# A fused attention and expert kernel: some key blocks' softmax sums by adding transfers, and an addition moved to GpSimd

## The chip, the cores and the metric

The kernel runs on one core of a Trainium2 chip. A time is the device time of one launch in microseconds (us); lower is better. The core has five engines that run their own instruction streams and meet at semaphores: TensorE (PE; its weight loads are shown apart as PEld), VectorE (DVE), ScalarE (ACT), GpSimd (POOL) and SyncE (SP, which only issues transfers). Sixteen DMA engines move the data. A transfer issued by SP or ScalarE is of the kind "hardware_dynamic" in the profile (queue q1 for SP), one issued by GpSimd is "software_dynamic" (queue q0).

## The reference

The kernel computes one block of a network in four parts. Only the third is touched by the change; the others matter as its neighbours.

```python
x = x + tanh(g_xattn[0]) * L0_xattn(layernorm(x), ctx, ...)      # projection and depooling
x = x + tanh(g_ffn[0])   * L0_ffn(layernorm(x), ...)             # 8 experts, top 1
# the third part: 2048 queries of 8 heads of 32 against 1601 keys
Q = split_heads(layernorm(x)) * 32 ** -0.5
K, V = split_heads(ctx[:, :256]), split_heads(ctx[:, 256:])
logits = einsum('bhqd,bhkd->bhqk', Q, K) + b + mask
x = x + tanh(g_xattn[1]) * softmax(logits) @ V
x = x + tanh(g_ffn[1])   * L1_ffn(layernorm(x), ...)             # 8 experts, top 2
```

## The kernel before

The attention is done in eight passes n = 0 to 7. A pass takes 512 queries (a group of four 128-row pieces) and four of the eight heads (hf = n % 2). The 1601 keys are 13 blocks kc of 128. In the function `interleaved`, which every engine walks through in its own way, a step is one key block of one pass, 8 x 13 steps and one more. In a step:

- TensorE makes four scores, one per head hh (`scores`, L587), 128 keys x 512 queries, into three PSUM banks in turn, so the fourth needs that ScalarE has emptied the first. ScalarE turns each into PT by an exp (L1315).
- PT is a ring of 16 buffers of 128 x 512, that is four key blocks: eight in Z1 and eight in WS0. The exp of a block waits until all readers of the block four before it have finished.
- One step later TensorE multiplies with the values of the block (`values`, L602, into PB6).
- The sum of the exps over all keys is needed too, for the division. For blocks 2, 4, 6, 8, 10 and 12 TensorE adds them up by a matmul with ones (`summed`, L592, into PB7). Blocks 0, 1, 3, 5, 7, 9 and 11 are first added up by GpSimd in ACC (L1468 for blocks 0 and 1, L1471 for the rest), 128 x 2048 per pass, and TensorE sums ACC at the end.
- In between, TensorE makes 402-column pieces of the scores of the next pass, whose row maxima VectorE takes (`maxima`, L569 and L1046), 64 pieces per pass. Their results go with the queries in QS. GpSimd prepares the query rows of the pass after that (`queries`, L1423 to L1427), four per pass.

At the end of a pass ScalarE copies PB6 and PB7 out (`attended`, L1321 and L1322), TensorE turns them (`turned_out`), and `into_x` puts the result into X in parts: part 0 the reciprocals of the sums (RT), part 1 the product with them (OT, L1072), part 2 gate times OT plus X (L1077), all on VectorE, and parts 4 to 7 the statistics of four rows. In pass 7 there are no maxima; instead VectorE prepares the rows for the last layer (`prepared`, L1102 to L1120), and after it TensorE begins with the router (L643 to L645). The order of the work is that of the code: each engine takes its instructions strictly as written, SP and GpSimd their transfers too.

The following lines show who waits for a block of the ring.

```python
# ScalarE, before the exp that overwrites block k of pass m
e.wait_ge(t_v, val_done(m, k, h))
if on_pool(k):
    e.wait_ge(p_acc, acc_done(m, k, h))
```

Of the kernel before, what the change touches and what calls it, by code (L numbers as in the profile page):

```python
# [76 lines left out]
def build(nc, cst, x, ctx_2048, plen, kmask, g_xattn, g_ffn, W_in, b_in, g_res, g_init, rw0, rb0, w01, w02,  # L77
          att_b, rw1, rb1, rw2, rb2, w11, w12, b12, out):
    es = ExitStack()
    with es:  # L80
# [111 lines left out]
        RW1 = Z0[:, 0:2048].rearrange("p (k n) -> p k n", k=2)  # L192
# [1474 lines left out]
```

## Time and profile before

| | us |
|---|---|
| median of 3 runs | 1227.48 (1226.67 to 1228.3) |
| the profiled execution | 1230.68 |
| its span, first to last instruction | 1228.9 |
| TensorE busy in it | 1099.3 (89%) |
| VectorE, ScalarE, GpSimd busy | 785.7, 532.3, 498.0 |
| mean granted clock of TensorE | 0.947 of full speed |

How the views read: a row of busy time by stretches has the stretch and its length, then for PE, PEld, DVE, ACT and POOL the busy us and in brackets the number of instructions, then the granted clock of TensorE (1.00 is full), the share of the DMA engines and GB/s. A row in order of time has start, duration (of the whole run of equal instructions, x of them), engine, line, operation, output<-inputs, and in square brackets the idle time ahead of it and what ended it. A group by line has busy us and mean ns of one, then the idle us before.

The span is cut into stretches by what the kernel does: the first layer's work until about 400 us, the attention until about 857 us, then the router and the last layer's experts. Pass 3 lies from about 590 to 646 us, pass 7 from about 812 to 857 us.

### The profile page before, as it was taken

The numbers are of one execution on the slowest core, as the hardware profiler recorded it, in microseconds if no ns is written. First come the engines' busy times: TensorE is split into PE (matmuls) and PEld (weight loads), VectorE is DVE, ScalarE is ACT, GpSimd is POOL, SyncE is SP. The second block draws the span as 40 slices with busy tenths as digits, with TensorE's granted clock in tenths as the row PEclk, the third lists the DMA queues.
The fourth block names the chain that finished last, engine by engine and source line by source line (L and its number), as shares of the span: only waits on it lengthen the run. The fifth ranks groups of instructions, "written<-read, shape, count | busy, mean of one in ns | idle before, by whom it ended". The sixth has DMA issues, their size and how long they took to land.

```text
span 1228.9 us, 20691 instructions
## 1 busy us (share of the span) xinstructions
PE 1099.3 (89%) x7126; PEld 826.5 (67%) x7126; DVE 785.7 (64%) x1804; ACT 532.3 (43%) x1145; POOL 498.0 (41%) x499
## 2 busy tenths in 40 slices
PE   4866999999967799999999999999983999999994
PEld 3665999999964444545455454544753999999994
DVE  5735767666659876767667676854339656565663
ACT  4141444433321345555565655565443333333341
POOL 1641111111104365857566676666002233434342
PEclk9966999999997889999999999999995999999998
DMA  6454787788832000000000000001623566666662
GB/s 225 94 148 182 317 318 289 302 322 336 339 131 86 1 1 1 1 18 1 1 1 18 2 1 2 18 22 50 220 73 112 162 181 211 183 208 198 192 210 57
DMA packets 52754, 160.71 MB, mean 131 GB/s; under 512 B 7434, under 2 KB 38540, under 8 KB 41644
## 3 DMA queue, kind: packets, MB, share of 16 engines
q1 hardware_dynamic: 38590, 138.42, 31.1%
q0 software_dynamic: 12000, 18.36, 6.4%
q10 hardware_dynamic: 2062, 2.60, 0.6%
q8 instruction: 60, 0.98, 0.3%
q14 instruction: 42, 0.34, 0.1%
HBM read 142.97 MB, written 16.38 MB: 130 GB/s over the span
## 4 chain that ended last, share of the span: by engine, by line
PE 78%; DVE 10%; issue 3%; ACT 2%; DMA 1%; POOL 1%; DVEq 0%; ACTq 0%; POOLq 0%
PE PQ L456 25%; PE PB L602 8%; PE PQ L587 7%; PE PB L483 6%; PE PB L569 5%; PE PB L592 4%; DVE Z L1046 4%; PE PB L332 4%; PE PB L502 3%; PE PQ L569 3%; PE PB L482 3%; PE PB L501 2%; PE PQ L643 1%; PE PQ L645 1%; PE PQ L644 1%
## 5 line engine op out<-in xcount | busy, mean ns | idle before, releaser
L1046 DVE TENSOR_REDUCE Z<-PB 128x1 f32<-128x402 f32 x319 | 172.3, 568 | 73.2 <-PE PB L569 71.6
L587 PE MATMUL PQ<-QS,KS 128*128 128x512 f32 x416 | 173.8, 433 | 3.3 <-ACT Z L1315 2.0
L456 PE MATMUL PQ<-Z,WS 128*128 128x128 f32 x1472 | 174.6, 278 | 0.5 <-ACT Z L1227 0.5
L456 PEld LDWEIGHTS PQ<-Z,WS 128*128 128x128 f32 x1472 | 173.1, 194 | 2.2 <-ACT Z L1227 0.9
L1242 ACT ACTIVATE Z<-PQ,W 128x128 f32<-128x128 f32 x312 | 89.0, 368 | 160.0 <-PE PQ L456 160.0
L456 PEld LDWEIGHTS PQ<-Z,W 128*128 128x128 f32 x1248 | 153.4, 194 | 4.8 <-ACT Z L1227 0.9
L456 PE MATMUL PQ<-Z,W 128*128 128x128 f32 x1248 | 154.3, 277 | 1.0 <-issue 0.5
L587 PEld LDWEIGHTS PQ<-QS,KS 128*128 128x128 f32 x416 | 77.1, 189 | 103.2 <-issue 67.7
L1315 ACT ACTIVATE Z<-PQ 128x512 f32<-128x512 f32 x208 | 109.8, 603 | 82.9 <-PE PQ L587 82.8
L1315 ACT ACTIVATE WS<-PQ 128x512 f32<-128x512 f32 x208 | 109.7, 604 | 82.6 <-PE PQ L587 82.4
L569 PE MATMUL PB<-KS,QS 128*128 128x402 f32 x319 | 119.1, 383 | 16.0 <-DVE Z L1046 7.0
L1046 DVE TENSOR_REDUCE Z<-PQ 128x1 f32<-128x402 f32 x193 | 106.9, 567 | 37.8 <-PE PQ L569 37.1
L1393 POOL DMA_INDIRECT out<-Z,SI x39 | 62.9, 1614 | 157.3 <-DMA out<-Z,SI 134.2
L1471 POOL TENSOR_TENSOR WS<-WS,Z 128x512 f32<-128x512 f32 x80 | 104.4, 1335 | 40.6 <-ACT Z L1315 40.6
L1386 POOL DMA_INDIRECT Z<-xn,SI x62 | 65.2, 1052 | 125.3 <-DVE SM L897 79.7
L1393 POOL DMA_INDIRECT yd<-Z,SI x23 | 22.6, 984 | 206.0 <-DVE Z L977 206.0
L569 PEld LDWEIGHTS PB<-KS,QS 128*128 128x128 f32 x319 | 61.2, 192 | 42.4 <-DVE Z L1046 27.9
L569 PE MATMUL PQ<-KS,QS 128*128 128x402 f32 x193 | 74.1, 398 | 7.0 <-DVE Z L1046 2.5
L1252 ACT ACTIVATE QS<-WS 128x1024 fp32r<-128x1024 f32 x46 | 48.6, 1057 | 71.3 <-PE PB L502 42.7
L502 PE MATMUL PB<-QS,AU 128*128 128x512 f32 x184 | 69.6, 406 | 0.0
L955 DVE CAST HP<-Z 128x256 fp32r<-128x256 f32 x78 | 25.0, 320 | 68.3 <-ACT Z L1242 68.3
L483 PE MATMUL PB<-W2F,HP 128*128 (+1 forms) x156 | 61.0, 413 | 0.0
(307 smaller groups left out, 2080.2 us busy)
## 6 DMA issues: line engine op xcount, KB each, us to landing
WS<-in_w SPq DMA_DIRECT2D x23, 2048.0 KB, 7.8
W<-in_w SPq DMA_DIRECT2D x39, 1028.0 KB, 5.1
WS<-in_w SPq DMA_DIRECT2D x23, 1024.0 KB
W2G<-in_w SPq DMA_DIRECT2D x8, 1024.0 KB, 9.3
xn<-WS SPq DMA_DIRECT2D x32, 128.0 KB, 1.8
X<-in_x SPq DMA_DIRECT2D x4, 512.0 KB, 12.1
WS<-yd SPq DMA_DIRECT2D x4, 512.0 KB, 5.1
out<-X SPq DMA_DIRECT2D x4, 512.0 KB, 2.8
```

What stands on the lines that cost most here:

```text
L456: t = e.matmul(bank[:, j * P:j * P + P], w[:, k, o:o + P], FXT[i % 2][:, k * P:k * P + P], start=k == 0, stop=k == 1)
L483: t = e.matmul(PB[6 + i % 2], hh[:, j * P:j * P + P], both, start=first, stop=n == 1 and j == 3)
L502: t = e.matmul(PB[6 + i % 2], HA[:, j * P:j * P + P], W2P[n][:, j, :, :].rearrange("p s n -> p (s n)"), start=first, stop=last)
L569: e.matmul(PB[b][:, 0:PIECE], q[:, h, t4 * P:t4 * P + P], KS[:, 4 * hf + h, s * PIECE:(s + 1) * PIECE], start=True, stop=True).then_inc(t_ ...
L587: e.matmul(PB[g % 3], KS[:, 4 * (n % 2) + hh, kc * P:kc * P + P], QS[n % 2][:, hh, :], start=True, stop=True).then_inc(t_s, 1)
L602: e.matmul(PB[6][32 * hh:32 * hh + 32, :], V[:, kc, (4 * hf + hh) * 32:(4 * hf + hh) * 32 + 32], PT[(g + hh) % 16], start=kc == 0, stop=kc ...
L1046: e.tensor_reduce(MP[j % 2][:, i:i + 1], PB[bank_of["pc", r]][:, 0:PIECE], AX.X, ALU.max).then_inc(v_pc, 1)
L1242: t = e.activation(FS[c % 4][:, j * P:j * P + P], PB[c % 4][:, j * P:j * P + P], ACT.Silu, bias=W1[i % 2][:, o:o + 1])
L1315: e.activation(PT[g % 16], PB[g % 3], ACT.Exp).then_inc(a_p, 1)
L1386: e.indirect_dma_start(FXL[i % 4], None, xn, bass.IndirectOffsetOnAxis(ap=tabi[:, i:i + 1].bitcast(U32), axis=0)).then_inc(d_xl[l][i % 4], 16)
L1393: e.indirect_dma_start(into, bass.IndirectOffsetOnAxis(ap=tabi[:, i:i + 1].bitcast(U32), axis=0), FY[i % 2], None, **add).then_inc(d_y[l][ ...
L1471: e.tensor_tensor(acc, acc, PT[g % 16], ALU.add).then_inc(p_acc, 1)
```

## The change

Five things change, all in the attention.

- Blocks 2, 4, 6 and 8 are no longer summed by TensorE. SP copies block 2 (all four heads, 128 x 2048) from the ring into a new accumulator ACCV by a transfer, once per pass. GpSimd issues, at the start of steps 5, 7 and 9, a transfer that adds block 4, 6 and 8 to ACCV (`accum_op`). Each waits until the exps of its block are done and the transfer before it has landed. TensorE sums ACCV at the end of the pass, before ACC. The exp that overwrites one of these blocks also waits for its transfer.
- ACCV takes the place where the router weights RW1 lay; RW1 moves to the place of QS, and its load moves from before the attention to pass 7, when the scores of pass 6 are done.
- The gate is multiplied into the reciprocals by a second small VectorE operation. The addition to X is done by GpSimd in step 3, as a plain addition.
- The statistics of rows, parts 4 to 7 of `into_x`, move from step 4 to steps 5, 7, 9 and 11, one in each.
- The 64 pieces of maxima per pass are spread as 6, 6, 4, 5, 5, 5, 5, 5, 5, 6, 6, 6 over steps 0 to 11, where they were 5, 5, 6 in turn.

```diff
+        RW1 = placed("RW1", [P, 2048], qs_at).rearrange("p (k n) -> p k n", k=2)
...
-        RW1 = Z0[:, 0:2048].rearrange("p (k n) -> p k n", k=2)
+        ACCV = Z0[:, 0:2048]
...
+        def block_of(n, kc):
+            q = (52 * n + 4 * kc) % 16
+            return Z1[:, 512 * q:512 * q + 2048] if q < 8 else WS[0][:, 512 * q - 2048:512 * q]
+
         def on_pool(kc):
             return kc == 0 or kc % 2 == 1
 
+        def added_in(n, kc):
+            return (d_acc, 16 * n + 16) if kc == 2 else (d_add, 48 * n + 8 * kc - 16)
+
+        def on_queue(kc):
+            return kc in (2, 4, 6, 8)
...
-            parts = {(2, 0): 0, (2, 1): 1, (3, 1): 2, (4, 0): 4, (4, 1): 5, (4, 2): 6, (4, 3): 7}
+            parts = {(2, 0): 0, (2, 1): 1, (3, 1): 2, (5, 1): 4, (7, 1): 5, (9, 1): 6, (11, 1): 7}
+            pieces = (6, 6, 4, 5, 5, 5, 5, 5, 5, 6, 6, 6)
...
-                left = (5, 5, 6)[kc % 3] if kc < NK - 1 else 0
+                left = pieces[kc] if kc < NK - 1 else 0
...
-                if not on_pool(kc):
-                    if kc == 2 and n:
+                if kc in (10, 12):
+                    if kc == 10 and n:
                         e.wait_ge(v_rt, n)
-                    summed(n, kc, kc == 2, False, lambda hh: PT[(g + hh) % 16])
+                    summed(n, kc, kc == 10, False, lambda hh: PT[(g + hh) % 16])
                 if kc == NK - 1:
+                    e.wait_ge(*added_in(n, 8))
+                    summed(n, kc, False, False, lambda hh: ACCV[:, 512 * hh:512 * hh + 512])
                     e.wait_ge(p_acc, acc_done(n, NK - 2, 3))
                     summed(n, kc, False, True, lambda hh: ACC[n % 2][:, 512 * hh:512 * hh + 512])
...
-                    e.reciprocal(RT, PB[7].rearrange("p (g d) -> p g d", d=32)[:, :, 0]).then_inc(v_rt, 1)
+                    vc.step(e, e.reciprocal(RT, PB[7].rearrange("p (g d) -> p g d", d=32)[:, :, 0]))
+                    e.tensor_scalar(RT, RT, tg[:, 1:2], None, ALU.mult).then_inc(v_rt, 1)
...
                     if on_pool(k):
                         e.wait_ge(p_acc, acc_done(m, k, h))
+                    if on_queue(k):
+                        e.wait_ge(*added_in(m, k))
...
+                if kc in (5, 7, 9) and hh == 0:
+                    e.wait_ge(a_p, 52 * n + 4 * kc)
+                    e.wait_ge(*added_in(n, kc - 3))
+                    e.dma_start(ACCV, block_of(n, kc - 1), accum_op=ALU.add).then_inc(d_add, 16)
...
+            def into_x(n, part):
+                if part == 2:
+                    qg, hf = divmod(n, 2)
+                    v = X[:, 4 * qg:4 * qg + 4, hf * P:hf * P + P]
+                    e.wait_ge(v_ot, n + 1)
+                    e.tensor_tensor(v, v, OT.rearrange("p (c d) -> p c d", c=4), ALU.add).then_inc(p_x3, 1)
...
-            e.dma_start(RW1, rw1.rearrange("(k p) n -> p k n", p=P)).then_inc(d_rw1, 16)
...
+            def first_block(n):
+                e.wait_ge(a_p, 52 * n + 12)
+                if n:
+                    e.wait_ge(t_v, 68 * n)
+                e.dma_start(ACCV, block_of(n, 2)).then_inc(d_acc, 16)
+
+            for n in range(7):
+                first_block(n)
+                if n in (2, 4, 6):
+                    finished(n // 2 - 1)
+            e.wait_ge(t_s, 364)
+            e.dma_start(RW1, rw1.rearrange("(k p) n -> p k n", p=P)).then_inc(d_rw1, 16)
+            first_block(7)
```

Two places show how the instructions move. Line numbers after the change are 13 to 17 higher. The first is on TensorE, at the end of pass 1: the values of block 12 (into PB6), the sums (into PB7, with CT's ones), and the first score of the next step. Before:

```order
L602 MATMUL PB6<-Z1_54,V_59 32x512 [waits a_p]
L602 MATMUL PB6<-Z1_54,V_59 32x512 x3
L592 MATMUL PB7<-Z1_54,CT_49 32x512 x4
L592 MATMUL PB7<-WS0_56,CT_49 32x512 [waits p_acc]
L592 MATMUL PB7<-WS0_56,CT_49 32x512 x3
L587 MATMUL PQ<-QS1_61,KS_58 128x512 [waits a_p]
```

After:

```order
L615 MATMUL PB6<-Z1_54,V_59 32x512 [waits a_p]
L615 MATMUL PB6<-Z1_54,V_59 32x512 x3
L605 MATMUL PB7<-Z1_54,CT_49 32x512 x4
L605 MATMUL PB7<-Z0_53,CT_49 32x512 [waits d_add]
L605 MATMUL PB7<-Z0_53,CT_49 32x512 x3
L605 MATMUL PB7<-WS0_56,CT_49 32x512 [waits p_acc]
L605 MATMUL PB7<-WS0_56,CT_49 32x512 x3
L600 MATMUL PQ<-QS1_61,KS_58 128x512 [waits a_p]
```

A third sum, over ACCV (Z0), has come in ahead of that over ACC (WS0), with a wait for the last adding transfer (d_add).

The second is on GpSimd in pass 2, steps 3 to 6: the adds of blocks 3 and 5 into ACC (here WS0), and one query row between them (L1423 and on). Before:

```order
L1471 TENSOR_TENSOR WS0_56<-WS0_56,Z1_54 128x512 [waits p_acc,a_p] x4
L1423 TENSOR_SCALAR Z0_53<-X_55,SM_50 128x128 [waits t_q,v_qn]
L1425 CAST AK1_63<-Z0_53 128x4x32 [waits p_own]
L1426 CAST AK1_63<-Z0_53 128x4x32
L1427 TENSOR_TENSOR AK1_63<-Z0_53,AK1_63 128x4x32 [waits p_own]
L1471 TENSOR_TENSOR WS0_56<-WS0_56 128x512 [waits p_acc,a_p] x4
```

After, with the issues of the first two adding transfers (L1476):

```order
L1488 TENSOR_TENSOR WS0_56<-WS0_56,Z1_54 128x512 [waits p_acc,a_p] x2
L1495 TENSOR_TENSOR X_55<-X_55,Z0_53 128x4x128 [waits v_ot]
L1488 TENSOR_TENSOR WS0_56<-WS0_56,Z1_54 128x512 [waits p_acc,a_p] x2
L1436 TENSOR_SCALAR Z0_53<-X_55,SM_50 128x128 [waits t_q,v_qn]
L1438 CAST AK1_64<-Z0_53 128x4x32 [waits p_own]
L1439 CAST AK1_64<-Z0_53 128x4x32
L1440 TENSOR_TENSOR AK1_64<-Z0_53,AK1_64 128x4x32 [waits p_own]
L1476 DMA Z0_53<-WS0_56 128x2048 [waits d_acc,a_p]
L1488 TENSOR_TENSOR WS0_56<-WS0_56 128x512 [waits p_acc,a_p] x4
L1476 DMA Z0_53<-Z1_54 128x2048 [waits d_add,a_p]
```

The addition to X stands in the middle of block 3's adds, the first adding transfer stands behind the query row, and the second behind block 5's adds, where it also waits for the first to land.

## Rows read from the trace of the kernel before

**Rows 1.** the page's busy times, with shares of the span

```profile
PE 1099.3 (89%) x7126; PEld 826.5 (67%) x7126; DVE 785.7 (64%) x1804; ACT 532.3 (43%) x1145; POOL 498.0 (41%) x499
```

**Rows 2.** busy time by stretches

```profile
425.00:480.00 55.00, 49.64 (x277) 24.30 (x269) 39.94 (x93) 26.92 (x51) 33.31 (x33) 0.94 0.00 1
...
580.00:630.00 50.00, 48.11 (x290) 24.78 (x288) 34.77 (x73) 28.86 (x56) 33.06 (x35) 1.00 0.00 1
...
830.00:856.00 26.00, 24.25 (x158) 8.84 (x148) 13.90 (x25) 14.46 (x28) 20.51 (x16) 1.00 0.11 37
```

**Rows 3.** the chain in order of time, attention: start, us, what

```profile
590.05 1.84 PE PB L592 x16
...
613.63 0.86 PE PB L592 x8
...
637.76 0.86 PE PB L592 x8
...
645.51 1.84 PE PB L592 x16
```

**Rows 4.** ScalarE in order of time, pass 3, blocks 3, 6, 8, 10, 12

```profile
602.29 2.07 ACT L1315 ACTIVATE WS<-PQ 128x512 f32<-128x512 f32 x4 [1.71 <-PE PQ L587]
...
614.96 2.07 ACT L1315 ACTIVATE Z<-PQ 128x512 f32<-128x512 f32 x4 [2.48 <-PE PQ L587]
...
623.07 2.06 ACT L1315 ACTIVATE WS<-PQ 128x512 f32<-128x512 f32 x4 [1.68 <-PE PQ L587]
...
630.84 2.06 ACT L1315 ACTIVATE Z<-PQ 128x512 f32<-128x512 f32 x4 [2.00 <-PE PQ L587]
...
639.09 0.60 ACT L1315 ACTIVATE WS<-PQ 128x512 f32<-128x512 f32 x1 [2.49 <-PE PQ L587]
```

**Rows 5.** TensorE in order of time, pass 3, scores of block 6

```profile
614.42 0.50 PE L587 MATMUL PQ<-QS,KS 128*128 128x512 f32 x1
...
615.76 0.39 PE L587 MATMUL PQ<-QS,KS 128*128 128x512 f32 x1
```

**Rows 6.** GpSimd in order of time, pass 3

```profile
602.96 5.46 POOL L1471 TENSOR_TENSOR WS<-WS,WS 128x512 f32<-128x512 f32 x4 [2.51 <-ACT WS L1315]
608.41 0.79 POOL L1423 TENSOR_SCALAR Z<-X,SM 128x128 f32<-128x128 f32 x1
...
609.88 0.46 POOL L1427 TENSOR_TENSOR AK<-Z,AK 128x128 fp32r<-128x128 f32 x1
```

**Rows 7.** GpSimd and VectorE in order of time, pass 7

```profile
821.86 5.05 POOL L1471 TENSOR_TENSOR WS<-WS,WS 128x512 f32<-128x512 f32 x4 [1.44 <-ACT WS L1315]
...
828.37 7.00 POOL L1471 TENSOR_TENSOR WS<-WS,Z 128x512 f32<-128x512 f32 x4 [1.46 <-ACT Z L1315]
...
832.04 2.19 DVE L1120 TENSOR_TENSOR KS<-Z,KS 128x1024 fp32r<-128x1024 f32 x1
```

**Rows 8.** the instructions on X, 50 to 106 us (ns), and landing

```profile
L1375 POOL DMA_INDIRECT X<-dep_d,SI x11: 1540/1542/1692, 48.8 to 70.8; - x11
...
DMA to landing us min/median/max: 3.6/3.8/4.1
```

**Rows 9.** DMA queues, 50 to 106 us: packets, MB, share of 16 engines

```profile
q0 software_dynamic: 1612, 1.46, 18.0%
```

**Rows 10.** the same view, 131 to 362 us

```profile
q1 hardware_dynamic: 5764, 62.93, 69.6%
q0 software_dynamic: 1968, 5.38, 5.9%
```

**Rows 11.** ScalarE in order of time, pass 7, blocks 3 and 12

```profile
821.19 2.07 ACT L1315 ACTIVATE WS<-PQ 128x512 f32<-128x512 f32 x4 [0.76 <-PE PQ L587]
...
851.36 2.07 ACT L1315 ACTIVATE WS<-PQ 128x512 f32<-128x512 f32 x4 [1.62 <-PE PQ L587]
```

**Rows 12.** groups of instructions by line, 500 to 940 us

```profile
L1077 DVE SCALAR_TENSOR_TENSOR X<-Z,SM,X 128x512 f32<-128x512 f32 x7 | 8.3, 1181 | 0.0
...
L1032 DVE TENSOR_REDUCE Z<-Z 128x4 f32<-128x16 f32 x23 | 3.9, 170 | 0.8
```

More of the change, by code:

```diff
@@ L247, in build @@
             sem(n) for n in ("v_x2", "v_qn", "p_q", "t_q", "a_q", "t_pc", "v_pc", "v_m", "t_m", "a_m"))
-        t_s, a_p, p_acc, t_v, a_ot, a_rec, t_rec, v_rt, t_ot, v_ot, v_x3 = (
-            sem(n) for n in ("t_s", "a_p", "p_acc", "t_v", "a_ot", "a_rec", "t_rec", "v_rt", "t_ot", "v_ot", "v_x3"))
+        t_s, a_p, p_acc, d_acc, d_add, t_v, a_ot, a_rec, t_rec, v_rt, t_ot, v_ot, p_x3 = (
+            sem(n) for n in ("t_s", "a_p", "p_acc", "d_acc", "d_add", "t_v", "a_ot", "a_rec", "t_rec", "v_rt", "t_ot", "v_ot", "p_x3"))
         t_xr, v_xr, v_xg, v_rw, t_hr, a_hr, t_lm, v_lt, t_lt = (
@@ L273, in val_done @@
         def val_done(n, kc, hh):
-            before = 80 * n + 4 * kc + 4 * max(0, (kc - 1) // 2)
-            return before + hh + (5 if kc and kc % 2 == 0 else 1)
+            before = 68 * n + 4 * kc + (4 if kc > 10 else 0)
+            return before + hh + (5 if kc in (10, 12) else 1)
         def acc_done(n, kc, hh):
             return 24 * n + 4 * (max(kc, 1) // 2) + hh + 1
+        def block_of(n, kc):
+            q = (52 * n + 4 * kc) % 16
+            return Z1[:, 512 * q:512 * q + 2048] if q < 8 else WS[0][:, 512 * q - 2048:512 * q]
         def on_pool(kc):
             return kc == 0 or kc % 2 == 1
+        def added_in(n, kc):
+            return (d_acc, 16 * n + 16) if kc == 2 else (d_add, 48 * n + 8 * kc - 16)
+        def on_queue(kc):
+            return kc in (2, 4, 6, 8)
         def interleaved(maxima, scores, values, attended, turned_out, into_x, prepared):
-            parts = {(2, 0): 0, (2, 1): 1, (3, 1): 2, (4, 0): 4, (4, 1): 5, (4, 2): 6, (4, 3): 7}
+            parts = {(2, 0): 0, (2, 1): 1, (3, 1): 2, (5, 1): 4, (7, 1): 5, (9, 1): 6, (11, 1): 7}
+            pieces = (6, 6, 4, 5, 5, 5, 5, 5, 5, 6, 6, 6)
             side = maxima(1)
@@ L1074, in into_x @@
                                     RT.unsqueeze(2).broadcast_to([P, 16, 32]), ALU.mult).then_inc(v_ot, 1)
-                elif part == 2:
-                    e.wait_ge(v_ot, n + 1)
-                    e.scalar_tensor_tensor(v, OT.rearrange("p (c d) -> p c d", c=4), tg[:, 1:2], v, ALU.mult,
-                                           ALU.add).then_inc(v_x3, 1)
                 elif part >= 4 and hf:
-                    e.wait_ge(v_x3, n + 1)
+                    e.wait_ge(p_x3, n + 1)
                     stats(4 * qg + part - 4)
@@ L1137, in _ @@
             inv_std(12, NC)
-            e.wait_ge(t_v, 640)
+            e.wait_ge(t_v, 544)
             def partial(g):
@@ L1471, in scores @@
                     e.tensor_tensor(acc, acc, PT[g % 16], ALU.add).then_inc(p_acc, 1)
-            interleaved(maxima, scores, lambda *a: None, lambda n: None, lambda n: None, lambda n, part: None, lambda c: None)
+            def into_x(n, part):
[4 more added lines that the diff above has]
+                    e.tensor_tensor(v, v, OT.rearrange("p (c d) -> p c d", c=4), ALU.add).then_inc(p_x3, 1)
+            interleaved(maxima, scores, lambda *a: None, lambda n: None, lambda n: None, into_x, lambda c: None)
+            into_x(7, 2)
             power(rst[:, 12:NC], 11)
@@ L1595, in stored @@
                     e.dma_start(xn1[(c + 1) * P:(c + 2) * P, :], XR[c % 4]).then_inc(d_xn[1][c % 4], 16)
-            for g in range(3):
-                finished(g)
+            def first_block(n):
[10 more added lines that the diff above has]
+            first_block(7)
             stored(0, 12)
-            e.wait_ge(t_v, 640)
+            e.wait_ge(t_v, 544)
+            e.wait_ge(v_rw, 2)
             def last_rows():
```

12 lines of the change are left out of this document (6 added, 6 removed).

## The prediction

> **What bounds the kernel now.** I read the page's busy times first, then the attention by stretches, then the chain, and last the instructions of one pass in order of time. Over the whole span TensorE is busy 89% and GpSimd 41% [rows 1]. The change lies in the attention, eight passes from about 425 us to 857 us. In a middle stretch of 50 us TensorE is busy 48.1 us, VectorE 34.8, ScalarE 28.9 and GpSimd 33.1, at full clock [rows 2]: TensorE sets the pace and every other engine has three tenths or more to spare. The chain [rows 3] shows what a change can take off it: a sum over a key block (four 32-column matmuls, shown as x8 at L592) is on the chain for 0.86 us, and at the end of a pass a double one for 1.84 us. From one pass end to the next it is 645.51 - 590.05 = 55.5 us, so one of 13 steps takes 4.3 us.
>
> **What it removes.** Per pass TensorE now makes seven such groups of sums: blocks 2, 4, 6, 8, 10, 12 and the GpSimd accumulator. After it makes four: 10, 12, the new accumulator ACCV and the old one. Three groups of 0.86 us are 2.58 us per pass, if the new work is never late. Eight passes give 20.6 us.
>
> **What it adds, and where it can be late.** Two things decide: how long one accumulating transfer takes (call it D, from the issue by GpSimd to landing), and when its result is needed. The buffer ring holds four blocks, so ScalarE can't write block 8 before the add of block 4 has landed, nor block 10 before that of 6, nor block 12 before that of 8. Besides, each add waits for the one before it, and that wait stands in GpSimd's queue, ahead of its own adds for blocks 7, 9 and 11 and of the next query rows; those have time (block 9's sum is needed four blocks on), so what counts is the ring.
>
> I count from the first exp of block 3 (602.29) in the pass of [rows 4]. Blocks 8, 10 and 12 begin at +20.8, +28.6 and +36.8. Without the sums of 2, 4, 6 (and 8, for the later two) they are due at 18.2, 25.1 and 33.4. The slack is small: TensorE's first score of a block starts at 614.42, the exp at 614.96 and takes some 0.6 us of a group of 2.07, and the fourth score, which needs that exp's bank, starts at 615.76 [rows 4, 5]. So 0.2 us, and the last due time is 33.6.
>
> GpSimd reaches the issue of add 4 this late: its adds of block 3 begin 0.67 us after the exp and take 5.05 us for four (rows of the last pass; 5.46 in this one, beside VectorE's update of x, which goes away), then the new addition to x, 1.3 us by the same adds, then the query rows, 608.41 to 610.34, 1.93 us [rows 6, 7]. Together 8.9 us. Then add 4 lands at 8.9 + D. Add 6 goes out when that has landed. Add 8 goes out when add 6 has landed, and not before GpSimd has spent 1.54 (issue [rows 8]) + 5.05 + 1.93 = 8.5 us on step 7. So add 8 lands at about 8.9 + D + max(D, 8.5) + D, to be held against 33.6. The block before, number 2, is copied by a plain transfer from SP, issued before +0 and due at 12.7 - 1.7 = 11 us; 2.9 + 2.8 us (below) hide in that.
>
> **D from both sides.** No row shows a 1 MB addition (128 x 8 KB). The nearest are 128 x 1 KB gathers that add into x: they land in 3.8 us, of which 1.54 is the issue [rows 8]. While 11 of them ran, the software queue took 18.0% of 16 engines over 56 us for 1.46 MB, that is 110 us of engine per MB [rows 9]. Without an addition the same queue took 5.9% over 231 us for 5.38 MB, 40.5 per MB, as the weight loads do (40.9) [rows 10]. A block is 1.05 MB, so on 16 engines 2.7 us at the plain rate and 7.2 us at the adding rate. The fixed part is 3.8 less eight rows of 0.113 us per engine: 2.9 us. Per row of 1 KB the addition costs 113 ns against 41. If the extra 72 ns are per row, eight rows of 8 KB take 8 x (8 x 41 + 72) = 3.2 us and D is 6.1. If they are per byte, D is 10.1. I take the middle, which is also what a second pass over the bytes with 30 ns left per row gives: 8 x (8 x 83 + 30) = 5.6 us, D = 8.4.
>
> The Trainium skill says why a transfer that adds is slower (Collectives: The Full Stack, section on the bandwidth ceiling): the addition costs nothing itself, but two operands are read through the same ring, so the rate halves, measured 1.93 times. The row shows 110/40.5 = 2.7 times for 1 KB rows, more than that. By the page D would be 2.9 + 2 x 2.7 = 8.2 us, and the pass would stall 0.2 us instead of the 0.6 below; by the row's full ratio it would be 10.1. This is an estimate from the page.
>
> **The sum.** Passes 1 to 6: add 8 lands at 8.9 + 8.4 + 8.5 + 8.4 = 34.2, 0.6 us late. Add 6, at 25.7 against 25.3, is late within the same 0.6. Gain 2.58 - 0.64 = 1.94, times 6: 11.6 us. Pass 0 has no addition to x (1.3 us earlier, so no stall) but TensorE waits elsewhere (49.6 busy of 55, clock 0.94 [rows 2]): 2.0 us of its 2.58.
>
> Pass 7 is the tight one. It has no maxima; blocks 3 to 12 take 851.36 - 821.19 = 30.2 us [rows 11], 26.7 without four sums, due 26.9. GpSimd is at 0.67 + 5.05 + 1.3 = 7.0 us when it issues, and its own step costs 6.6 us, less than D, so the last add lands at 7.0 + 3 x 8.4 = 32.2: 5.3 us late, which turns the 2.58 gained into a loss of 2.7 us. TensorE is busy 24.3 of 26 us there [rows 2], so nothing else swallows it.
>
> Gate: the reciprocals get a dependent second small operation, which a 128x16 row prices at 0.17 us [rows 12]; TensorE waits for the result once per pass, so 7 x 0.15 = 1.0 us. The other edits I cost at nothing. VectorE loses 1.18 us per pass [rows 12] and has time. The spread of the maxima keeps 64 pieces per pass in steps with at least four each; if VectorE trailed, each extra piece would cost its 0.5 us. The router weights are fetched at pass 7's start and first read four steps later, some 13 us at pass 7's pace of 30.2 us for nine, against 5.7 us by the terms above; without that cover VectorE would wait up to the difference, but only its own preparation hangs on it.
>
> 11.6 + 2.0 - 2.7 - 1.0 = 9.9 us. The profiled execution took 1230.7 us (span 1228.9), 3 us over the median of 1227.5. Its sum is 1220.8, and for the median **1217.6, say 1217 us**. The sum is zero at D = 8.9 and moves by 2.4 us for each 0.1 us of D, since eight passes hold three adds each.
>
> **Rivals.**
> (a) All hidden. If the extra is per row, D = 6.1: passes 1 to 6 give 15.5, pass 0 and 7 2.6 each, less 1.0: 1208 us. For it: the extra was seen on 1 KB rows only. Against: 2.7 times is too much for a start-up cost on transfers whose plain kind shows none. Chance 0.2.
> (b) The adding transfers become the bound, slower than before. One mechanism: at D = 10.1, where the row's rate per byte holds, the last add lands at 8.9 + 30.3 = 39.2, 5.6 us late, in passes 1 to 6 (+3.1 net each, 18.4), 4.3 late in pass 0 (+1.8) and 10.4 in pass 7 (+7.8), plus 1.0: 29 us, 1256 us. It decides from D = 8.9 on. For it: the row measured on this very kind of addition, into the same memory. Against: nothing but the row length. Chance 0.35 for any D above 8.97.
> (c) The added time equals the removed one, D of 8.8 to 8.97: 1225 to 1230 us. Chance 0.05.
> (d) GpSimd can't issue in time. In pass 7 four adds took 7.00 us instead of 5.05 with a two-input operation of VectorE of 2.19 us beside them [rows 7]. If each pass-7 issue met such an operation, 1 to 2 us each, 3 to 6 us in all, the time would be 1221 to 1223. It only adds to the others; chance as the deciding one 0.05, inside my forecast. The Trainium skill has a rule for it (SBUF — State Buffer, section on the two separate sides): while VectorE holds the shared port pair, GpSimd can't write the descriptors of its transfers, and they seem blocked. In the middle passes VectorE mostly reduces from PSUM, so I give the rule no more.
> My forecast itself (D of 7 to 8.8, 1208 to 1225 us) has 0.40, with (d) in it.
>
> **Range and chances.** Small D and mine together 0.60, no change 0.05, slower 0.35. Differences below 0.2% (2.5 us) a measurement of this kernel can't tell from none. The range must hold 8 in 10, so it takes in (a) and nearly all of (b): 1206 to 1255 us.
>
> **What the changed profile would show.** Right: the L592 groups fall from seven to four per pass (the line has moved by 13); the software queue moves 25 MB more, at 70 to 90 us of engine per MB; the accumulating issue lands in 8 to 8.8 us; ScalarE's exp of block 12 waits under 1 us for a transfer in the middle passes and about 5 us in pass 7; the pass takes some 53.6 us. Wrong: landings above 8.9 us, GpSimd idle before its second and third issue, and ScalarE waiting at blocks 8, 10 and 12 of every pass. If instead TensorE waits at the sum of ACCV, or VectorE is what TensorE waits for, the place of the loss is another than I have named.

## The result

The change makes the kernel slower: 1274.89 us (median of 5 runs, 1270.78 to 1276.11) against 1226.67 (5 runs, 1225.93 to 1228.3) of the kernel before beside it. The ratio is 1.0378 with a 95% interval of 1.036 to 1.0395. That is 46 us by the ratio, where I had forecast a gain of 10. The profiled execution took 1275.43 us, its span is 1273.6.

**The transfers are not the cause.** The page's row for GpSimd's queue (packets, MB, share of 16 engines) and its DMA issues (KB each, us to landing), kernel after:

```profile
q0 software_dynamic: 15456, 43.53, 15.8%
...
Z<-Z POOLq DMA_DIRECT2D x12, 1024.0 KB, 6.9
Z<-WS POOLq DMA_DIRECT2D x12, 1024.0 KB, 6.9
```

The 24 adding transfers land 6.9 us after their issue, between my two ends (6.1 and 10.1) and 1.5 us better than the 8.4 that I took. ScalarE, whose exps I expected to be late, hardly waits for them. Who waited for the adding transfers in the whole kernel (us, times), and their landing. Seven waits are of GpSimd's next issues, and one is of an exp, 0.8 us:

```profile
  POOL Z L1476: 11.1, 7
  ACT WS L1328: 0.8, 1
DMA to landing us min/median/max: 6.8/6.9/8.7
```

**Where the time went.** I cut passes 1 to 7 at ScalarE's copy of PB6. The last line is the sum over all seven, kernel before first:

```profile
591.90:647.40 55.50, 53.60 (x317) 28.32 (x317) 38.13 (x79) 32.49 (x63) 37.53 (x40) 1.00 0.00 1
...
sum 376.20, PE 360.53 PEld 184.16 DVE 257.18 ACT 220.05 POOL 256.11; mean PE 51.50 PEld 26.31 DVE 36.74 ACT 31.44 POOL 36.59
```

and the kernel after:

```profile
608.50:668.20 59.70, 52.55 (x293) 28.82 (x293) 40.64 (x79) 32.73 (x62) 40.99 (x44) 0.97 0.31 71
...
729.50:791.60 62.10, 55.04 (x293) 29.49 (x293) 40.47 (x79) 32.83 (x62) 41.02 (x44) 0.92 0.29 68
...
sum 413.30, PE 358.80 PEld 187.32 DVE 272.96 ACT 221.71 POOL 278.93; mean PE 51.26 PEld 26.76 DVE 38.99 ACT 31.67 POOL 39.85
```

The seven passes take 413.3 us instead of 376.2, 37.1 more. TensorE has 24 matmuls fewer in a full pass (x293 for x317), as said, but over the seven passes it is busy only 1.7 us less, and it stands idle 54.5 us (413.3 - 358.8) instead of 15.7. Two things, then: it waits 38.8 us more, and its granted clock (the mean over a pass), 1.00 in every pass before, is 0.92 to 0.97 after, so that fewer matmuls take nearly as long. What it waits for, 540 to 860 us (us in total, times, longest), after:

```profile
PE PB L582 <- DVE Z L1061: 15.2, 9, 3.5
PE PB L582 <- DVE Z L1087: 10.0, 4, 2.5
PE PQ L582 <- DVE Z L1061: 9.4, 5, 3.5
PE PQ L582 <- DVE Z L1087: 2.5, 1, 2.5
```

L1061 is VectorE's maximum of a piece, L1087 its product OT. A maxima matmul (L582) needs the PSUM bank that VectorE empties. Before, the same view has 0.6 us for the maxima and 6.0 for the product (1.2 each); now it is 24.6 and 12.5. VectorE is late although it is busy two thirds of the time: some of its small operations take long. VectorE and GpSimd in order of time, pass 3, after:

```profile
614.38 0.25 DVE L1082 RECIPROCAL Z<-PB 128x16 f32<-128x16 f32 x1
614.67 1.18 DVE L1083 TENSOR_SCALAR Z<-Z,SM 128x16 f32<-128x16 f32 x1
...
616.25 0.68 DVE L1087 TENSOR_TENSOR Z<-PB,Z 128x512 f32<-128x512 f32 x1
...
628.16 0.92 POOL L1476 DMA_DIRECT2D Z<-WS  x1
628.82 5.25 POOL L1488 TENSOR_TENSOR WS<-WS,Z 128x512 f32<-128x512 f32 x4
...
630.87 3.23 DVE L1049 TENSOR_TENSOR AU<-Z,AU 128x4 fp32r<-128x4 f32 x1
634.02 1.04 DVE L1061 TENSOR_REDUCE Z<-PB 128x1 f32<-128x402 f32 x2
```

TensorE in the same pass, all its rows that waited for VectorE:

```profile
616.98 0.45 PE L582 MATMUL PB<-KS,QS 128*128 128x402 f32 x1 [2.49 <-DVE Z L1087]
...
634.64 0.45 PE L582 MATMUL PB<-KS,QS 128*128 128x402 f32 x1 [3.45 <-DVE Z L1061]
...
647.96 0.45 PE L582 MATMUL PB<-KS,QS 128*128 128x402 f32 x1 [0.79 <-DVE Z L1061]
```

The reader sees three places. The gate multiplication L1083, 16 numbers per partition, takes 1.18 us, about one GpSimd add (1.28); the product begins that much later. The last operation of the maxima's split, L1049, takes 3.23 us. (The split is the three small operations that follow every sixteenth piece; this one has four numbers per partition.) It ends at 634.1, with GpSimd's whole run of four adds (628.82 + 5.25), which stands directly behind an adding transfer's issue. And there is a third wait of 0.8 us, without a long operation. Over the kernel L1049 takes (ns min/median/max):

```profile
L1049 DVE TENSOR_TENSOR AU<-Z,AU x32: 167/430/5766, 383.7 to 843.4; 128x4 fp32r<-128x4 f32 x32
```

Each of the passes 1 to 6 has one such operation of 3.0 to 3.3 us, and each of the six ends 0.03 to 0.04 us after the last of the adds behind an issue. Three others in these passes (at 535.34, 657.55 and 780.93) fall beside four adds with no issue ahead of them, and take 0.96 to 0.98. The one of 5.77 us is in pass 0.

Pass 7 has no maxima, but the same thing happens to VectorE's preparation of rows. Its addition L1131 and the wait of TensorE behind it:

```profile
867.08 6.33 DVE L1131 TENSOR_TENSOR KS<-RW,KS 128x1024 fp32r<-128x1024 f32 x1
```

```profile
873.80 0.69 PE L345 MATMUL PB<-CT,WS 128*128 128x128 f32 x2 [4.61 <-DVE WS L1113]
```

The kernel before makes this addition twice, in 1.23 us and in the 2.19 us of [rows 7]; now it is 6.33 and 1.23. Now an adding transfer is issued at 866.44 and four adds follow it until 872.32.

Three suspects, one for each part of the change: (A) the issue on GpSimd, (G) the gate's multiplication on VectorE, (P) the new places of the maxima. The router weights' new place has no run of its own. It is in all the kernels below, and the two cheapest of those without transfers (gate_copy_only and stats_only) cost about 2 us each.

### The profile page after: what moved, and what is told of

It is laid out like the page before. It is cut to its first block, busy times and chain, and to the rows that moved or that the text cites. A ratio compares the mean times of both kernels' runs of the same rounds, so it can differ in the third digit from the quotient of the medians.

```text
span 1273.6 us, 20379 instructions
## 1 busy us (share of the span) xinstructions
PE 1100.5 (86%) x6934; PEld 832.5 (65%) x6934; DVE 807.4 (63%) x1804; ACT 535.3 (42%) x1145; POOL 526.2 (41%) x531
## 4 chain that ended last, share of the span: by engine, by line
PE 75%; DVE 12%; issue 5%; ACT 2%; DMA 1%; POOL 1%; SPq 0%; ACTq 0%; DVEq 0%; POOLq 0%
PE PQ L469 24%; PE PB L615 8%; PE PQ L600 7%; PE PB L496 5%; DVE Z L1061 5%; PE PB L582 5%; PE PB L345 4%; PE PB L515 3%; PE PQ L582 3%; PE PB L495 3%; PE PB L605 2%; PE PB L514 2%; PE PQ L658 1%; PE PQ L660 1%; PE PQ L659 1%
## 5 line engine op out<-in xcount | busy, mean ns | idle before, releaser
L1061 DVE TENSOR_REDUCE Z<-PB 128x1 f32<-128x402 f32 x319 | 173.0, 568 | 84.7 <-PE PB L582 83.5
L600 PE MATMUL PQ<-QS,KS 128*128 128x512 f32 x416 | 182.0, 453 | 3.1 <-ACT Z L1328 2.0
L582 PE MATMUL PB<-KS,QS 128*128 128x402 f32 x319 | 124.0, 399 | 44.1 <-DVE Z L1061 31.8
L600 PEld LDWEIGHTS PQ<-QS,KS 128*128 128x128 f32 x416 | 81.5, 200 | 109.8 <-issue 54.7
L1061 DVE TENSOR_REDUCE Z<-PQ 128x1 f32<-128x402 f32 x193 | 106.9, 568 | 43.6 <-PE PQ L582 43.2
L1488 POOL TENSOR_TENSOR WS<-WS,Z 128x512 f32<-128x512 f32 x80 | 101.6, 1338 | 34.7 <-ACT Z L1328 34.6
L582 PEld LDWEIGHTS PB<-KS,QS 128*128 128x128 f32 x319 | 64.2, 202 | 71.6 <-DVE Z L1061 52.7
L582 PE MATMUL PQ<-KS,QS 128*128 128x402 f32 x193 | 75.9, 408 | 16.9 <-DVE Z L1061 10.7
L582 PEld LDWEIGHTS PQ<-KS,QS 128*128 128x128 f32 x193 | 40.1, 210 | 32.6 <-DVE Z L1061 24.7
```

Of the source, the lines that this page charges most:

```text
L582: e.matmul(PB[b][:, 0:PIECE], q[:, h, t4 * P:t4 * P + P], KS[:, 4 * hf + h, s * PIECE:(s + 1) * PIECE], start=True, stop=True).then_inc(t_ ...
L600: e.matmul(PB[g % 3], KS[:, 4 * (n % 2) + hh, kc * P:kc * P + P], QS[n % 2][:, hh, :], start=True, stop=True).then_inc(t_s, 1)
L1061: e.tensor_reduce(MP[j % 2][:, i:i + 1], PB[bank_of["pc", r]][:, 0:PIECE], AX.X, ALU.max).then_inc(v_pc, 1)
L1488: e.tensor_tensor(acc, acc, PT[g % 16], ALU.add).then_inc(p_acc, 1)
```

## Experiments

Twelve kernels in four series, each beside runs of the kernel before on the same chip. Their medians were 1227.46 us (transfers_only, rest_only, resync, sp_copies), 1225.51 (memset_no_wait, gate_only, spread_only, resync_old_rest), 1228.73 (gate_copy_only, resync_gate_old_spread) and 1226.37 (pieces_only, stats_only). Where I give a cost in us and no two rows, it is the ratio less one, times 1227 us; its uncertainty is about 2 us either way, as the intervals show, and that of a difference of two such costs about 3. The recorded ratio is not that of the two medians and differs from it by up to 0.15%.

Where a run is called "the kernel before with" something, it was built from the changed kernel: transfers and new sums are out, the named parts are in, and the router weights stay at their new place with their load in pass 7.

### The transfers alone, and all but the transfers

transfers_only keeps the diff's transfers and sums, with the gate, the addition to x, the statistics and the pieces as before. rest_only is the reverse: all six even blocks are summed by TensorE again.

```diff
 transfers_only, against the changed kernel
...
-            pieces = (6, 6, 4, 5, 5, 5, 5, 5, 5, 6, 6, 6)
+            pieces = (5, 5, 6, 5, 5, 6, 5, 5, 6, 5, 5, 6)
-                    e.tensor_scalar(RT, RT, tg[:, 1:2], None, ALU.mult).then_inc(v_rt, 1)
...
 rest_only, against the changed kernel
-            return kc in (2, 4, 6, 8)
+            return False
...
```

> The changed kernel with the rest as before: gate and addition to x on VectorE, statistics in step 4, maxima 5, 5, 6. Theory A: the transfers take 2.6 us per pass off TensorE, but one VectorE operation of 3 us or more per pass stays where it falls into the adds behind an issue, about 5 us with the clock that falls: 1240 to 1260 us. If the pieces fall elsewhere the operation may miss the adds in most passes, then 1215 to 1225. Theory B: 1207 to 1215 us.

> The changed kernel without its transfers: TensorE sums blocks 2, 4, 6 and 8 again, nothing is copied or added into ACCV; gate in the reciprocals, addition to x on GpSimd, statistics and maxima spread as changed. Theory A (VectorE's operations on SBUF are shut out by GpSimd's adds, worst in the four adds right behind the issue of a transfer): no 3 us operation on VectorE is left, but the gate's small multiplication still takes 1.2 us and TensorE waits 2.5 us for the product behind it once per pass, so 7 x 1.3 us and some lost clock: 1236 to 1243 us. Theory B (the transfers are innocent, the spread of maxima and statistics makes VectorE late): as slow as the whole change or slower, 1265 us or more, since the three sums come back on top.

transfers_only: 1227.89 us (1224.08 to 1230.07), ratio 0.9999 [0.9984, 1.0015]: no change. rest_only: 1253.63 (1252.17 to 1254.91), 1.0212 [1.0193, 1.0231]. So the transfers by themselves bring nothing and cost nothing, and the rest costs 26 us. Neither result lies in a range that I had written: 26 us is above theory A's 9 to 16 and below theory B's 38, and transfers_only lies between the two branches of A. Together they would be 26 us; the change loses 46. The two parts make each other worse by about 20 us.

transfers_only's zero is a gain and a loss. Its passes 1, 3 and 4, by stretches:

```profile
476.10:531.80 55.70, 51.78 (x293) 27.47 (x293) 39.69 (x79) 32.61 (x63) 40.08 (x43) 1.00 0.33 77
...
586.40:643.60 57.20, 53.28 (x293) 28.69 (x293) 39.78 (x79) 32.77 (x63) 40.09 (x43) 0.97 0.32 74
643.60:698.10 54.50, 51.98 (x293) 27.46 (x293) 38.96 (x87) 32.57 (x63) 40.12 (x43) 1.00 0.36 88
```

Pass 4 is 1.7 us shorter than before (54.5 for 56.2). In each of the odd passes 1, 3 and 5 stands one L1049 of 2.73 us, with a wait of 1.9 us of TensorE behind it. Passes 1 and 5 are 0.2 and 0.3 us longer than before, at a clock of 1.00: the wait has taken what the sums gave. Pass 3 with the same wait is 1.7 us longer, at 0.97. In the changed kernel a long operation stands in each of the passes 1 to 6: the moved maxima bring a split beside the adds behind an issue every time. Most of the 20 us comes from there, as the runs with a wait behind the issue show (below).

### What makes VectorE's small operation long

resync puts a tiny GpSimd operation behind each issue and waits for its completion before the adds. memset_no_wait has a like operation, on a column of its own, without the wait. sp_copies takes the issues off GpSimd in passes 0 to 6: SP makes plain copies at the same points, so the accumulator holds only the last block (this leaves three of the four blocks out of the sums).

```diff
 resync
                     e.dma_start(ACCV, block_of(n, kc - 1), accum_op=ALU.add).then_inc(d_add, 16)
+                    pc.step(e, e.memset(nh[:, 0:1], -0.5))
 memset_no_wait
+                    i = 3 * n + (kc - 5) // 2
+                    e.memset(spare[:, i:i + 1], 0.0)
...
 sp_copies, on SP
+                for kc in (5, 7, 9) if n < 7 else ():
+                    e.wait_ge(a_p, 52 * n + 4 * kc)
+                    e.wait_ge(*added_in(n, kc - 3))
+                    e.dma_start(ACCV, block_of(n, kc - 1)).then_inc(d_add, 16)
```

> The changed kernel with one small GpSimd memset behind each adding transfer's issue, on whose completion GpSimd waits before its adds. Theory A, that in the adds which directly follow an issue GpSimd leaves VectorE no gap between them: with the wait in between, the long operation (3.0 to 5.8 us) is 1.2 us at most again, TensorE's 3.2 to 3.5 us wait once per pass falls under 1 us, and the time is 1232 to 1245 us; GpSimd loses 3 x 0.5 us per pass, which it has. Theory C, that the transfer in flight (6.9 us) shuts VectorE out: the long operation stays at 3 us, 1273 to 1280 us.

> The changed kernel with the adding transfers of passes 0 to 6 replaced by plain copies of the same blocks into ACCV, issued by SP; so the sums of blocks 2, 4 and 6 are left out there. Pass 7 keeps its adding transfers. Theory A: no issue on GpSimd, so no long operation on VectorE in passes 0 to 6: 1230 to 1242 us, as with the wait behind the issue. Theory C (bytes moving through SBUF shut VectorE out): three more copies of 4.5 us each are in flight in a pass, and the long operation stays near 2 to 3 us, 1255 us or more.

> The changed kernel with the same small GpSimd memset behind each adding issue, but no wait for it. Theory A (the adds that follow an issue without a meeting point leave VectorE no gap): only the wait mends it, so the long VectorE operation stays at 3 us or more once per pass and the time is 1272 to 1280 us. Theory D (the wait only moved the adds in time, by half a us, and so past the operation): the memset moves them alike, and the time is 1240 to 1250 us.

resync: 1242.5 us (1242.33 to 1242.8), 1.0125 [1.0107, 1.0143]. sp_copies: 1243.15 (1241.5 to 1245.51), 1.0126 [1.0104, 1.0149]. memset_no_wait: 1271.57 (1268.9 to 1273.31), 1.037 [1.0349, 1.0391]. The same rows in resync, pass 3, with the memset between:

```profile
614.43 0.92 POOL L1476 DMA_DIRECT2D Z<-WS  x1
615.06 0.42 POOL L1477 MEMSET SM<- 128x1 f32 x1
615.56 4.98 POOL L1489 TENSOR_TENSOR WS<-WS,Z 128x512 f32<-128x512 f32 x4
...
617.12 0.99 DVE L1049 TENSOR_TENSOR AU<-Z,AU 128x4 fp32r<-128x4 f32 x1
```

and the durations of that operation over the kernel (ns min/median/max), resync and then memset_no_wait:

```profile
L1049 DVE TENSOR_TENSOR AU<-Z,AU x32: 166/172/1315, 383.5 to 813.8; 128x4 fp32r<-128x4 f32 x32
```

```profile
L1050 DVE TENSOR_TENSOR AU<-Z,AU x32: 166/424/5856, 382.1 to 839.5; 128x4 fp32r<-128x4 f32 x32
```

The adds begin 0.08 us after the memset's end here; in the changed kernel they began 0.26 us before the issue's end (628.82 against 628.16 + 0.92), as far as spans on GpSimd can be trusted. The wait for GpSimd's own completion is worth 31 us. The memset alone does nothing (45 us lost as against 46), and with the issues gone from GpSimd in passes 0 to 6 (sp_copies, longest L1050 1.07 us) the effect is gone there too, although four adds in a row still run. A transfer in flight is not enough, since in resync the transfers fly as before. sp_copies has its own control in pass 7, which keeps its issues: VectorE's addition of 128x1024 takes 6.42 us there, as in the changed kernel (6.33), and TensorE waits 4.71 us behind it; in resync it takes 2.19. The rows of that line (ns min/median/max), sp_copies and then resync:

```profile
L1132 DVE TENSOR_TENSOR KS<-RW,KS x2: 1225/3821/6417, 840.2 to 848.4; 128x1024 fp32r<-128x1024 f32 x2
```

```profile
L1131 DVE TENSOR_TENSOR KS<-RW,KS x2: 2183/2184/2185, 836.2 to 841.5; 128x1024 fp32r<-128x1024 f32 x2
```

So it needs both: an issue, and adds behind it that are not held back. Then VectorE's two-input operation waits for the end of the run of adds; otherwise for about one add. Resync lies in its expected range; sp_copies is 1.2 us above its own and memset_no_wait 0.4 below, which changes neither reading.

### The gate and the addition to x

gate_only is the kernel before with the gate in the reciprocals and the addition to x on GpSimd (that edit is left out here). gate_copy_only moves the gate elsewhere, as a scale in ScalarE's copy.

```diff
 gate_only, against the kernel before
-                    e.reciprocal(RT, PB[7].rearrange("p (g d) -> p g d", d=32)[:, :, 0]).then_inc(v_rt, 1)
+                    vc.step(e, e.reciprocal(RT, PB[7].rearrange("p (g d) -> p g d", d=32)[:, :, 0]))
+                    e.tensor_scalar(RT, RT, tg[:, 1:2], None, ALU.mult).then_inc(v_rt, 1)
...
 gate_copy_only, against gate_only
-                    e.tensor_scalar(RT, RT, tg[:, 1:2], None, ALU.mult).then_inc(v_rt, 1)
...
-                e.activation(OT, PB[6], ACT.Copy).then_inc(a_ot, 1)
+                e.activation(OT, PB[6], ACT.Copy, scale=tg[:, 1:2]).then_inc(a_ot, 1)
```

> The kernel before with two edits only: gate multiplied into the reciprocals, addition to x on GpSimd. Theory A: the small multiplication reads and writes SBUF and waits for a GpSimd add, 1.18 us, so the product behind it is 1.2 us later and TensorE waits 2.5 us for it instead of 1.2, in seven passes, plus up to 0.9 us of lost clock each: 1236 to 1243 us. Rival (VectorE's relief of 1.2 us per pass makes up for it): 1225 to 1229 us.

> The kernel before with one part of the change, the add to x on GpSimd, and with the gate moved not into the reciprocals but into ScalarE's copy of the turned-out block (a scale of an operation that is there anyway); sums, pieces and statistics as before. It splits the 19.5 us that gate_only showed. Theory G: the loss is the small gate multiplication on VectorE, which waits 1.2 us for a GpSimd add and holds back the product and TensorE behind it. Then this kernel takes 1224 to 1232 us, and the product's start is back where it was. Theory X: the loss comes from the add to x on GpSimd, which is now one more GpSimd operation that reads SBUF and stands ahead of the running sums. Then it takes 1238 to 1248 us.

gate_only: 1245.88 us (1244.22 to 1247.05), 1.0151 [1.0131, 1.0171]. gate_copy_only: 1230.74 (1228.05 to 1234.81), 1.0016 [0.9999, 1.0033]. By the ratios that is 18.5 us (the 19.5 of an expectation is not the ratio's) and 2.0. gate_only is above its range of 1236 to 1243, gate_copy_only inside that of theory G, which holds: the addition to x on GpSimd costs some 2 us, not clear of none, and about 16.5 are one multiplication of 16 numbers per partition and pass. VectorE and TensorE of gate_only, pass 3:

```profile
600.41 0.25 DVE L1080 RECIPROCAL Z<-PB 128x16 f32<-128x16 f32 x1
600.70 1.04 DVE L1081 TENSOR_SCALAR Z<-Z,SM 128x16 f32<-128x16 f32 x1
...
602.14 0.67 DVE L1085 TENSOR_TENSOR Z<-PQ,Z 128x512 f32<-128x512 f32 x1
```

```profile
602.87 0.55 PE L582 MATMUL PQ<-KS,QS 128*128 128x402 f32 x1 [2.35 <-DVE Z L1085]
```

and passes 1, 3 and 4 by stretches:

```profile
479.10:535.60 56.50, 53.47 (x317) 28.22 (x317) 37.93 (x79) 32.43 (x62) 38.25 (x41) 1.00 0.00 1
...
594.40:652.20 57.80, 54.85 (x317) 28.82 (x317) 38.03 (x79) 32.49 (x62) 38.25 (x41) 0.97 0.00 1
652.20:710.70 58.50, 55.24 (x317) 28.81 (x318) 39.80 (x87) 32.47 (x62) 38.29 (x41) 0.97 0.03 10
```

The wait grows from 1.21 to 2.35 us. Pass 3 grows by 2.3 us, though: TensorE is busy 1.25 us longer for the same 317 matmuls, at a granted clock of 0.97 where the kernel before and gate_copy_only have 1.00. Pass 1 separates the two: with the same wait, at a clock of 1.00, it grows by 1.0 us. So about half of the price of the gate is the clock, which was lower in five of the six passes where TensorE waits 2.35 us and in none of those where it waits 1.21.

### The places of the maxima and statistics

```diff
 spread_only, pieces_only, against the kernel before
+            pieces = (6, 6, 4, 5, 5, 5, 5, 5, 5, 6, 6, 6)
-                left = (5, 5, 6)[kc % 3] if kc < NK - 1 else 0
+                left = pieces[kc] if kc < NK - 1 else 0
 spread_only, stats_only
-            parts = {(2, 0): 0, (2, 1): 1, (3, 1): 2, (4, 0): 4, (4, 1): 5, (4, 2): 6, (4, 3): 7}
+            parts = {(2, 0): 0, (2, 1): 1, (3, 1): 2, (5, 1): 4, (7, 1): 5, (9, 1): 6, (11, 1): 7}
```

> The kernel before with the spread only: maxima 6, 6, 4, 5, 5, 5, 5, 5, 5, 6, 6, 6 and statistics in steps 5, 7, 9 and 11. The run with gate and spread together was 26 us slower; what the gate doesn't explain must be here. If the effects add up and the gate costs 9 to 16 us: 1237 to 1245 us. If the spread costs nothing (my prediction's assumption): 1225 to 1229 us.

> The kernel before with the changed division of the maxima pieces alone (6, 6, 4, 5, 5, 5, 5, 5, 5, 6, 6, 6 in the place of 5, 5, 6 over and over); statistics after step 4 as before. With stats_only it splits the 14 us of spread_only. Theory P: the pieces cost it, since they put two further pieces into a step and the groups of small operations of VectorE's split at other places against the maxima matmuls that wait for a free bank; then 1236 to 1243 us here and 1226 to 1231 us for stats_only. Theory S: the statistics cost it, 0.6 us of VectorE each, four times in odd passes' followers, now between maxima of steps 5, 7, 9 and 11; then 1226 to 1231 us here.

> The kernel before with the statistics of the blocks of x moved from step 4 to steps 5, 7, 9 and 11 alone; pieces of the maxima as before. Theory S: 1236 to 1243 us, and half of it only in the passes that have statistics. Theory P: 1226 to 1231 us, as four operations of 0.4 us and four of 0.2 us every second pass are the same work in another place.

spread_only: 1240.28 us (1238.88 to 1242.61), 1.0112 [1.0089, 1.0136]. pieces_only: 1236.34 (1234.53 to 1237.75), 1.0085 [1.0065, 1.0105]. stats_only: 1228.86 (1226.48 to 1231.35), 1.0017 [1.0004, 1.003]. That is 13.7, 10.4 and 2.1 us. Theory P holds: the pieces carry most of it. In pieces_only, pass 3, VectorE and TensorE around the second split:

```profile
616.98 0.17 DVE L1045 TENSOR_REDUCE Z<-Z 128x4 f32<-128x16 f32 x1
...
617.26 0.57 DVE L1047 TENSOR_TENSOR AU<-Z,AU 128x4 fp32r<-128x4 f32 x1
```

```profile
618.37 0.45 PE L582 MATMUL PB<-KS,QS 128*128 128x402 f32 x1 [0.80 <-DVE Z L1059]
618.76 1.07 PE L615 MATMUL PB<-Z,V 128*32 128x512 f32 x8
```

A split follows each sixteenth piece. With 5, 5, 6 the sixteenth is always the last of its step, and while VectorE splits, TensorE does values and sums (L602, L592), which need no bank of it. With the new division two splits in a pass fall among the scores and pieces of a step, and in pass 3 TensorE waits 0.80 and 0.78 us. The number of pieces per step, which I had looked at, does not show this; where the sixteenth falls does. Passes 1 to 5 are 1.6 to 1.7 us longer and pass 6 is 1.2, at a clock of 1.00, and these two waits are 1.6 us of it.

### The transfers without the three costs

resync_old_rest is transfers_only with the waited-for memset. resync_gate_old_spread adds to it the addition to x on GpSimd and the gate as a scale of ScalarE's copy.

> The transfers alone, gate, addition to x, statistics and maxima as before, with the memset and the wait behind each issue. Theory A: the transfers without the wait gave no difference, with a VectorE operation of 2.7 us and a TensorE wait of 1.9 us per pass; without these and with the clock kept, 2 to 3 us per pass come back: 1207 to 1216 us. Rival: the gain of the removed sums is taken by something else as well (VectorE paces the passes), then 1222 to 1228 us.

> The transfers with the waited-for memset behind each issue, maxima and statistics as before, the gate in ScalarE's copy and the add to x on GpSimd: all of the change that the runs so far don't speak against, with the gate's small operation taken off VectorE. Against resync_old_rest (1219.7 us) it differs by the gate and the add to x alone. Theory G: 1214 to 1221 us, since VectorE loses one operation of some 0.7 us a pass and gains none. Theory X: 1230 to 1242 us.

resync_old_rest: 1219.74 us (1219.14 to 1220.34), 0.9943 [0.9924, 0.9962]. That is a gain of 7.0 us where transfers_only had none, but less than I expected (1207 to 1216). resync_gate_old_spread: 1216.9 (5 runs, 1214.26 to 1218.45), 0.9892 [0.9872, 0.9911], as expected: 11.8 us less than the kernel before beside it by the medians, 13.3 by the ratio. Passes 3, 4 and 7 of it, and the sum of 1 to 7:

```profile
585.90:638.90 53.00, 50.99 (x293) 27.57 (x294) 35.73 (x78) 32.56 (x62) 41.24 (x47) 1.00 0.34 80
638.90:694.00 55.10, 51.68 (x293) 27.58 (x293) 38.42 (x86) 32.55 (x62) 41.31 (x47) 1.00 0.36 87
...
800.10:844.80 44.70, 38.38 (x217) 15.15 (x217) 23.73 (x40) 25.89 (x51) 36.56 (x31) 0.96 0.51 130
sum 366.90, PE 344.88 PEld 179.01 DVE 245.07 ACT 220.66 POOL 282.84; mean PE 49.27 PEld 25.57 DVE 35.01 ACT 31.52 POOL 40.41
```

Pass 3 is 2.5 us shorter than before, nearly the three sums that I had counted (2.58). The even passes, with the statistics, give 1.1 to 1.9. In resync_old_rest, with the addition to x on VectorE, passes 1 to 6 give only 1.2 to 1.7 each. What comes off TensorE therefore comes off the pass only as far as VectorE lets it. Pass 7 is 2.0 us longer, and it is in gate_copy_only as well (44.7 us, without transfers): TensorE waits 2.1 us in one place in both for the rows that VectorE prepares, and 0.2 there before the change. In gate_copy_only VectorE's first copy and addition of 128x1024 in that stage take 1.63 and 2.19 us beside GpSimd's adds, against 0.68 and 1.23 before, 1.9 us together. That the moved addition to x, which shifts the adds, brings them together is argued and not tested.

## Why the prediction was wrong

- **The sums.** "Three groups of 0.86 us are 2.58 us per pass": right as TensorE's work. x317 becomes x293, and TensorE is busy 2.6 us less in pass 3 of resync_gate_old_spread (50.99 for 53.60). The pass gets 2.5 us of it at best and 1.1 in an even pass, though, so "eight passes give 20.6 us" was too much even without the losses; "VectorE ... has time" was what I had not shown.
- **D.** I took 8.4 us, and 6.9 was measured, nearer to the rate per row (6.1) than I had put it. Put into my own sum, 8.9 + 6.9 + 8.5 + 6.9 = 31.2 us is before the 33.6 at which add 8 is due: nothing late in passes 1 to 6, and in the trace one exp of pass 2 waits 0.8 us for a transfer and no other exp does. In the stretch 500 to 860 us the software queue moves 18.88 MB at 25.5% of 16 engines, which is 0.255 x 360 x 16 / 18.88 = 78 us of engine per MB, inside the 70 to 90. With 6.9 for 8.4 the prediction's own sum would have been 15.5 + 2.0 + 1.8 - 1.0 = 18.3 us of gain, about 1209 us by my estimate, further from the result. The whole argument on rival (b) was over a term that did not decide. (The slope of 2.4 us for each 0.1 us of D holds only above D = 8.5, where three landings count in a pass; below it two count.)
- **The failed step: "Gate: ... a dependent second small operation, which a 128x16 row prices at 0.17 us", 1.0 us in all.** Measured: 16.5 us (gate_only less gate_copy_only, 18.5 - 2.0). I took the price from a reduction, which never waits for GpSimd here (0.17 us in all 32 cases); the multiplication reads and writes SBUF too, and took 1.18 us where 0.23 is its shortest. The kernel before had a row of the other kind: L1034, four numbers per partition, 0.58 us on the mean of 500 to 940 us and 0.97 at 613.90 beside GpSimd's adds.
- **The second failed step: "The other edits I cost at nothing", "the spread of the maxima keeps 64 pieces".** Measured: 14 us, 10 of them from the pieces, and through them the transfers' long operations in every pass instead of every second. I counted the pieces and not where the split falls.
- **The third, a term that the sum did not have, near rival (d), "GpSimd can't issue in time".** I had the right pair of engines and looked in the wrong direction. I asked how VectorE delays GpSimd's issue, and confined it to pass 7. What happens is that GpSimd's adds behind the issue hold VectorE, in every pass: 31 us (the change less resync, 46.4 - 15.3). The sentence "if VectorE is what TensorE waits for, the place of the loss is another than I have named" is what came true.
- **Pass 7.** I forecast 2.7 us lost by late adds; 3.7 are lost (46.4 for 42.7). No exp of pass 7 waits for a transfer. TensorE waits there for VectorE, 4.61 us at once.

The parts do not add up one by one, since the waits lie in the same passes and the clock answers to them together: gate 18.5 and spread 13.7 give 26.0 together (rest_only). But the transfers' part of the loss goes with the wait behind the issue: rest_only's 26.0 less resync_old_rest's gain of 7.0 would be 19.0, and resync has 15.3, where without the wait 26.0 and 0 became 46.4. What holds is a chain of ratios: 1.0378 (all), 1.0125 (with resync, 31 us less), 0.9943 (gate, addition to x and spread as before, 22 less), 0.9892 (gate in ScalarE's copy, addition to x on GpSimd, 6 less).

What is not shown is why the adds behind an issue close VectorE out. The Trainium skill (GPSIMD Engine Reference, section on instruction dispatch) states that consecutive instructions of this engine are no barrier between its cores, each of which takes the next instruction when its own share is done. A guess built on it is that after an issue the cores are out of step, so that at no moment all of them are between two adds, and that a wait for completion brings them together. The runs fit it (memset without a wait 1271.6, with it 1242.5) but no view shows the cores, and the guess stays one.

## What to carry to other kernels

Price a small operation by a row of the same kind, with its inputs in the same memories and beside the same neighbour engine, and at its longest, not at its mean: one of 16 numbers per partition, eight times in the kernel, cost 16.5 us here. Before moving work in a hand-ordered interleaving, ask what stands after the n-th piece and whose bank it holds back. And when GpSimd issues transfers between its own adds, let it wait for its own completion once behind each issue, or keep VectorE's two-input operations out of the adds behind.

## What the runs showed of the hardware

- A VectorE operation with two SBUF inputs waits for GpSimd's two-input adds: in the kernel before, the one of four numbers takes 0.17 us alone and up to 1.18 beside adds of 1.28 us each. The Trainium skill (SBUF — State Buffer, section on who interferes with whom) has this as a lock held for one instruction. By that rule, with adds of 1.3 us, I would estimate no wait above 1.3 us. That fits the kernel before. In the changed kernel the operation takes 3.23 us, and 5.77 at most, when the adds follow an issue: here the measurement decides.
- A multiplication of 128x16 by a scalar, SBUF to SBUF, takes 0.23 to 1.19 us in the changed kernel. Reductions over SBUF inputs of the same size (L1047, 0.17 us) don't wait.
- An adding transfer of 1 MB from SBUF to SBUF lands in 6.9 us, 0.9 of it GpSimd's issue; a plain one issued by SP lands in 4.5.
- The granted clock of a pass, a mean over its stretch, was 1.00 in all of the passes 1 to 6 without a wait of TensorE above 1.3 us (before, gate_copy_only, pieces_only, spread_only, stats_only and the two last runs). Where the longest wait was 2.35 to 2.5 us (gate_only, rest_only, resync, sp_copies) it was 0.97 in 17 of 24 passes and 1.00 in 7, so the length of one wait does not settle it. In the changed kernel, with 2.5 and up to 3.5, it was 0.92 to 0.97. I estimate the slower clock at some 11 us of the change's loss: TensorE was busy 358.8 us in passes 1 to 7, and 347.9 in resync_old_rest with the same matmuls at 1.00 but for pass 7.
